# Sums of four steps for the softmax denominators, a part of the adds on VectorE, and the router's weight product moved, in a one-core attention and expert kernel

## The chip, the cores and the metric

The kernel runs on one core of a Trainium2 chip. The metric is the device time of one execution in microseconds (us), the median of several runs. TensorE multiplies matrices; VectorE, ScalarE and GpSimd work element by element, and SyncE issues the transfers (DMAs). Each engine has its own queue of instructions, worked off in order, and they meet only in semaphores.

## What is computed

A graph attention layer over 2048 nodes, then a causal attention of 16 heads, then a router and eight experts (the two best for each token). The part that matters here:

```python
scores = jnp.einsum('bhqd,bhkd->bhqk', q, k) / jnp.sqrt(jnp.float32(HD))
scores = jnp.where(causal, scores, -jnp.inf)
attn = jax.nn.softmax(scores, axis=-1)          # exp(s - max) / sum of them
y = jnp.einsum('bhqk,bhkd->bhqd', attn, v)
x = x + y @ w_o
logits = xf.astype(jnp.float32) @ w_router.astype(jnp.float32)   # xf: x, normed with g2
```

The layer norm ahead of the attention treats the 2048 rows as one sequence: 16 tiles of 128, 16 heads of 32 columns, 512 columns in all.

## The kernel before

**Stages.** `stage_sequence` (norm, x @ W_seq, the adjacency matrix turned), `stage_factors` (a short stage of small tiles), `stage_masks` (graph attention), `stage_front` (projections), `stage_attention`, `stage_slots` (who goes to which expert), `stage_experts`. A stage is one block: the next begins when every engine has ended its part.

**Attention.** The heads go in four quads of four. A quad has NS = 40 steps, in chunks c = 0 to 3 of 512 queries: chunk c has 4c + 4 steps, one for each 128 keys; its last four are the diagonal ones, whose columns begin at 0, 128, 256 and 384. In each step n TensorE makes the scores of step n + 1 in two halves z of two heads (`scores`, L1639 and L1642), ScalarE exponentiates them into one of three buffers E[n % 3] (L1407), and TensorE multiplies the values with E (`values`, L1653, four heads side by side in the array, two records each).

The denominator is the sum of E over all keys. GpSimd first adds the E of two steps, 2k and 2k + 1, into `total` (L1369; where the second step is narrower, a copy, L1368, takes over the first columns), and TensorE then multiplies `total` with ones (`denominators`, L1666), accumulating in one bank through a chunk. There is one `total`: GpSimd waits for `den_done` before the next pair. ScalarE's exponential into E[n % 3] waits until step n - 3 has been multiplied and summed. In the second half of the last quad VectorE makes the half z = 1 of the pair's add (`pair_sum`, L1535 and L1536).

**Score maxima.** The exponentials need the maximum of each row. TensorE makes the scores of a query tile against up to 512 keys (`entry`, L1622, with L1625 on the diagonal) in one of two banks, and VectorE takes the maximum (L1473). So TensorE may be two maxima ahead of VectorE. In steps 0 to 20 of a quad the maxima of its own later chunks are made, in steps 21 to 39 those of the next quad, some four a step (more in the first quad); TensorE spreads them around the two score halves: a quarter of them, scores z = 0, up to a half, scores z = 1, the rest, then `denominators`, then `values`. VectorE's queue has for each step: the maxima, the copy of a finished chunk (L1433), one part of a divide (a reciprocal, L1451, and a multiply, L1445, of 128 columns; five parts for each chunk, from four steps behind its end), then `pair_sum` where it is VectorE's.

**Last quad, second half.** No maxima are left. Behind steps 23 to 35 TensorE makes the output products and the router's (`router`: "out" L1699, "share" L1703, "sum" L1708) for 12 of 16 tiles, VectorE adds them up (L1482, L1486) and GpSimd adds the rows to the residual (`add_row`, L1356). Behind the last denominators product come four "out" jobs; the first needs the divide of the last chunk.

**Router's weight product.** The logits' weights are g2 times w_router; `stage_factors` multiplies them with w_o, in 16 products of 128 x 8 columns (L390), after its own transposes (L383), and ScalarE copies the result to WG (L367). Its inputs are the last DMAs of `stage_sequence`; GpSimd multiplies them with g2 (L325).

## Time and profile before

| | us |
|---|---|
| median of three runs | 2271.41 (2270.23 to 2273.5) |
| the profiled execution | 2268.96 |
| its span, first to last instruction | 2267.2 |
| TensorE busy | 2055.1 (91%) |
| VectorE busy | 1553.6 (69%) |
| ScalarE busy | 1078.9 (48%) |
| GpSimd busy | 584.4 (26%) |

One execution is recorded by the profiler. Busy shares are means over stages with different bounds, so each stage has to be read by itself. A product's line gives its duration from start to end; products overlap, so what one costs TensorE is the distance from its start to the next start. "idle before" tells how long an engine had nothing to do ahead of an instruction, and who ended that. The granted clock of TensorE is 1.00 at 2.4 GHz and 0.50 at 1.2 GHz.

### The profile page before, as it was taken

The page shows a single profiled execution, that of the slowest core. Times are in us where ns is not written, and L with a number is a line of the kernel's source. Part 1 is how long each engine was busy: PE and PEld are TensorE (multiplying, and loading weights), DVE is VectorE, ACT ScalarE, POOL GpSimd, SP SyncE. Part 2 cuts the span into 40 slices and gives each one's busy share as a digit, 9 for nine tenths or more (in the row PEclk, how much of TensorE's full clock was granted, in tenths as well). Part 3 has the DMA queues.
Part 4 walks back from the last instruction along what each step waited for, and adds up shares of the span by engine and source line. Part 5 has one row for each costly group of instructions (what it writes and reads, how often), then busy time and mean ns, then how long its engine had stood idle before and what let it go on. Part 6 is the DMA issues. An engine that isn't in the chain of part 4 may idle for free. (4 is left out here: it accounts for less than half of the span.)

```text
span 2267.2 us, 42225 instructions
## 1 busy us (share of the span) xinstructions
PE 2055.1 (91%) x17716; PEld 1213.2 (54%) x17716; DVE 1553.6 (69%) x2563; ACT 1078.9 (48%) x1059; POOL 584.4 (26%) x447
## 2 busy tenths in 40 slices
PE   6899999999996899989999999999991599999997
PEld 3554444444442344544444444444430599999997
DVE  6679999999984666757777778768347544444442
ACT  4868988989890333213444444444430233323331
POOL 2610000000002012333454555555340222222211
PEclk8989999999998999969999999999995699999999
DMA  6521212212115013343103121010203444444431
GB/s 227 182 79 51 72 52 74 69 52 78 49 52 199 25 47 102 130 112 72 36 16 87 31 64 49 20 38 10 80 24 130 158 121 121 121 121 121 116 66 24
DMA packets 90905, 185.87 MB, mean 82 GB/s; under 512 B 14332, under 2 KB 23548, under 8 KB 86332
## 3 DMA queue, kind: packets, MB, share of 16 engines
q1 hardware_dynamic: 81756, 162.20, 21.8%
q0 software_dynamic: 8960, 20.98, 5.0%
q8 instruction: 140, 2.29, 0.4%
q14 instruction: 49, 0.40, 0.1%
HBM read 138.47 MB, written 40.23 MB: 79 GB/s over the span
## 5 line engine op out<-in xcount | busy, mean ns | idle before, releaser
L1473 DVE TENSOR_REDUCE t_rm<-t_m 128x1 f32<-128x512 f32 (+3 forms) x640 | 372.8, 605 | 150.2 <-PE t_m L1622 96.8
L1407 ACT ACTIVATE t_E<-t_s 128x1024 f32<-128x1024 f32 (+3 forms) x320 | 277.4, 895 | 412.3 <-PE t_s L1639 223.8
L1369 POOL TENSOR_TENSOR t_total<-t_E 128x1024 f32<-128x1024 f32 (+2 forms) x151 | 292.4, 1947 | 221.4 <-PE t_d L1666 215.6
L573 ACT ACTIVATE m_step<-m_ub,gat_bias 128x2048 bf16<-128x2048 f32 x128 | 250.0, 1989 | 11.1 <-DMA m_ub<-scratch_uac 5.7
L715 PE MATMUL m_bd<-m_mask,m_S 128*32 128x512 bf16 x3072 | 230.4, 379 | 10.9 <-DVE m_mask L663 10.9
L715 PE MATMUL m_bd<-gat_adjT,m_S 128*32 128x512 bf16 x2496 | 201.4, 379 | 4.8 <-PE m_dn L715 4.8
L715 PE MATMUL m_bd<-m_mask,m_neg 128*32 128x512 bf16 x2496 | 189.0, 379 | 0.0
L1996 POOL DMA_INDIRECT out<-e_ye,e_token x40 | 80.7, 2018 | 339.1 <-DVE e_ye L2099 334.4
L2160 PE MATMUL e_h<-e_xTh,e_w1h 128*128 128x320 f32 x512 | 159.1, 311 | 1.4 <-DVE e_xTl L2080 1.4
L2160 PE MATMUL e_h<-e_xTh,e_w1l 128*128 128x320 f32 x512 | 158.8, 310 | 0.0
L2160 PE MATMUL e_h<-e_xTl,e_w1h 128*128 128x320 f32 x512 | 158.8, 310 | 0.0
L663 DVE TENSOR_TENSOR m_mask<-m_step,gat_adjT 128x2048 bf16<-128x2048 bf16 x128 | 153.3, 1219 | 4.0 <-PE m_dn L715 2.2
L1653 PE MATMUL t_o<-t_E,k_rows 128*32 128x512 f32 (+3 forms) x1280 | 153.2, 552 | 0.0
L900 POOL MEMSET k_triq<- 128x128 bf16 x1 | 0.2, 206 | 574.3 <-POOLq L2221 574.3
L2091 DVE SCALAR_TENSOR_TENSOR e_hTl<-e_h,e_hTh 128x320 fp32r<-128x320 f32 x128 | 62.7, 490 | 116.0 <-ACT e_hTh L2045 116.0
L715 PEld LDWEIGHTS m_bd<-m_mask,m_S 128*32 128x32 bf16 x3072 | 89.9, 96 | 95.3 <-DVE m_mask L663 25.2
L573 ACT ACTIVATE k_rows<-m_ub,gat_bias 128x2048 bf16<-128x2048 f32 x64 | 126.7, 1993 | 28.0 <-DVE m_mask L663 28.0
L573 ACT ACTIVATE gat_seq<-m_ub,gat_bias 128x2048 bf16<-128x2048 f32 x64 | 126.7, 1992 | 27.2 <-DVE m_mask L663 27.2
L1622 PE MATMUL t_m<-t_K,tq_Q 96*128 96x512 f32 (+3 forms) x288 | 121.5, 438 | 16.3 <-DVE t_rm L1473 14.1
L2179 PE MATMUL e_y<-e_w2h,e_hTh 128*128 128x512 f32 x320 | 127.5, 398 | 0.0
L2179 PE MATMUL e_y<-e_w2l,e_hTh 128*128 128x512 f32 x320 | 125.0, 391 | 0.0
L2179 PE MATMUL e_y<-e_w2h,e_hTl 128*128 128x512 f32 x320 | 124.7, 390 | 0.0
(359 smaller groups left out, 4085.7 us busy)
## 6 DMA issues: line engine op xcount, KB each, us to landing
a_adj<-in_adj SPq DMA_DIRECT2D x16, 1024.0 KB, 4.9
m_ub<-scratch_uac SPq DMA_DIRECT2D x16, 1024.0 KB, 5.0
e_w1r<-in_L_ffn_w SPq DMA_DIRECT2D x8, 2048.0 KB, 8.2
e_w2r<-in_L_ffn_w SPq DMA_DIRECT2D x8, 2048.0 KB, 8.8
tq_Q<-scratch_parts SPq DMA_DIRECT2D x36, 256.0 KB, 4.6
gat_scale<-scratch_uac SPq DMA_DIRECT2D x32, 256.0 KB
scratch_parts<-o_hi SPq DMA_DIRECT2D x32, 256.0 KB, 2.2
scratch_parts<-o_lo SPq DMA_DIRECT2D x32, 256.0 KB, 2.7
```

The costliest lines, as they stand in the source:

```text
L573: act.activation(step(n), ub[h % 2][:, :].rearrange("p (t q) -> p t q", t=T), ACT.Relu, bias=bias[:, j, h:h + 1], scale=BIG).then_inc(step ...
L663: dve.tensor_tensor(mask[n % MASKS][:, :].rearrange("p (t q) -> p t q", t=T), step(n), adjT[:, j, :].rearrange("p (t q) -> p t q", t=T), A ...
L715: return pe.matmul(out[c * TILE:(c + 1) * TILE, :], lhs, rhs[:, c * BANK:(c + 1) * BANK], **flags)
L1369: pool.tensor_tensor(total[:, two, off:BANK], E[a % 3][:, two, off:BANK], E[(a + 1) % 3][:, two, off:BANK], ALU.add).then_inc(summed[z], 1)
L1407: act.activation(E[n % 3][:, two, off:BANK], ps_s[:, two, off:BANK], ACT.Exp, scale=SCALE).then_inc(exp_done[z], 1)
L1473: dve.tensor_reduce(rm[:, h, t, ch:ch + 1], ps_m[i % 2][:, 0:w], AX, ALU.max).then_inc(entry_read, 1)
L1622: mm = pe.matmul(ps_m[i % 2][:, 0:w], Q[c][0:ROWS, h, t % 4 * P:(t % 4 + 1) * P], K[q % 2][ch][0:ROWS, h, 0:w], start=True, stop=not diag)
L1653: mm = pe.matmul(ps_o[h * DH:(h + 1) * DH, off:BANK], V[:, kt, (q * G + h) * DH:(q * G + h + 1) * DH], E[n % 3][:, h, off:BANK], start=(kt ...
L1996: pool.indirect_dma_start(out=out, out_offset=bass.IndirectOffsetOnAxis(ap=token[e % 3][:, s:s + 1], axis=0), in_=ye[s % 2][:, :], in_offs ...
L2091: dve.scalar_tensor_tensor(hT[1][:, f, cut], ps_h[n % 4][:, 0:HC], 0.0, hT[0][:, f, cut].bitcast(F32), ALU.max, ALU.subtract).then_inc(h_r ...
L2160: mm = pe.matmul(ps_h[n % 4][:, 0:HC], w1s[wp][:, k, f * P:(f + 1) * P], xT[xp][:, k, half * HC:(half + 1) * HC], start=(m == 0), stop=(m ...
L2179: mm = pe.matmul(ps_y[s % 2][:, :], hT[hp][:, f, s * P:(s + 1) * P], w2s[wp][:, f, :], start=(m == 0), stop=(m == 3 * FK - 1))
```

## The change

`denominators` now runs once for four steps, over the full 512 columns. The sum is built step by step: at the second step of a group of four the E of the first two are added into `total`, at the third and fourth E is added to `total`. The wait for `den_done` stands at the second step, and step 4k + 5 of TensorE holds the product of group k. VectorE makes the half z = 1 of the fourth step of each full group before step 144, at its place in step n + 1 (LAST_BY_VECTOR), and all halves z = 1 from step 144 on (BY_VECTOR). ScalarE's exponential waits for the sum up to step n - 3. GpSimd's row additions come a step later. Of the router's weight product, two of four column blocks move to the end of `stage_sequence`, behind a product with g2 that GpSimd now makes ahead of its products for tile 14, and a ScalarE copy; the third goes ahead of the first transposes of `stage_factors`, the fourth ahead of the transposes that wait for the exponentials. A PSUM bank of its own (`late`) holds these two.

```diff
@@ stage_sequence
+def router_columns(pe, keep, bank, k):
+    for b in range(KD):
+        mm = pe.matmul(bank[:, EXPERTS * k:EXPERTS * (k + 1)], keep["woT"][:, b, k * P:(k + 1) * P],
+                       keep["G"][:, b, :], start=(b == 0), stop=(b == KD - 1))
+    return mm
...
+                pool.memset(keep["WG"][:, :, :], 0.0).then_inc(g_ready, 1)
                 pool.wait_ge(a_in, 32)
                 for t in range(T - 1):
+                    if t == T - 2:
+                        pool.wait_ge(late_in, 16 * (KD + 2))
+                        pool.tensor_tensor(keep["G"][:, :, :], keep["G"][:, :, :],
+                                           keep["g2"][:, :, None].to_broadcast([P, KD, EXPERTS]),
+                                           ALU.mult).then_inc(g_ready, 1)
...
                 store(T - 1)
+                act.wait_ge(wg_early, WG_EARLY)
+                act.activation(keep["WG"][:, 0:WG_EARLY, 0:EXPERTS],
+                               ps_t[0][:, 0:WG_EARLY * EXPERTS].rearrange("p (k e) -> p k e", k=WG_EARLY), ACT.Copy)
...
                 turn(T - 1)
+                pe.wait_ge(g_ready, 2)
+                for k in range(WG_EARLY):
+                    router_columns(pe, keep, ps_t[0], k).then_inc(wg_early, 1)
@@ stage_factors
                     if n == 0:
+                        router_columns(pe, keep, late, WG_EARLY).then_inc(wg_full, 1)
                         pe.wait_ge(u_ready, 1)
                     if n == 2:
+                        for k in range(WG_EARLY + 1, KD):
+                            router_columns(pe, keep, late, k).then_inc(wg_full, 1)
                         pe.wait_ge(exp_done, 1)
...
-                pe.wait_ge(g_ready, KD + 3)
-                for k in range(KD):
-                    for b in range(KD):
...
@@ stage_attention
+    FOUR = 4
+    SUMS = []
+    for n in range(QUADS * NS):
+        first_pair = 2 if STEPS[n % NS - n % FOUR + 1][2] else 1
+        SUMS.append((SUMS[-1] if n else 0) + (first_pair, 0, 1, 1)[n % FOUR])
...
+    BY_VECTOR = range((QUADS - 1) * NS + HALF + FOUR, QUADS * NS)
+    LAST_BY_VECTOR = [n for n in range(BY_VECTOR.start) if n % FOUR == 3 and STEPS[n % NS][2] == 0]
...
+        def add_step(eng, n, z):
+
+            off, two = STEPS[n % NS][2], slice(2 * z, 2 * z + 2)
+            eng.wait_ge(exp_done[z], n + 1)
+            if n % FOUR == 1:
+                if n >= FOUR:
+                    eng.wait_ge(den_done, n // FOUR)
+                if off:
+                    eng.tensor_copy(total[:, two, 0:off], E[(n - 1) % 3][:, two, 0:off]).then_inc(summed[z], 1)
+                before = E[(n - 1) % 3]
+            else:
+                eng.wait_ge(summed[z], SUMS[n - 1])
+                before = total
+            eng.tensor_tensor(total[:, two, off:BANK], before[:, two, off:BANK],
+                              E[n % 3][:, two, off:BANK], ALU.add).then_inc(summed[z], 1)
...
+                for n in range(QUADS * NS):
+                    if n % FOUR:
+                        for z in range(1 if n in BY_VECTOR or n in LAST_BY_VECTOR else 2):
+                            add_step(pool, n, z)
+                    if n >= (QUADS - 1) * NS:
+                        while added < EARLY and STEP_OF[added] < n % NS - 2:
                             add_row(added)
                             added += 1
...
-                            act.wait_ge(summed[z], SUMS[(n - 3) // 2 + 1])
+                            act.wait_ge(summed[z], SUMS[n - 3])
...
-                        if s % 2 and (q * NS + s) // 2 in BY_VECTOR:
-                            pair_sum((q * NS + s) // 2)
+                        if q * NS + s - 1 in LAST_BY_VECTOR:
+                            add_step(dve, q * NS + s - 1, 1)
+                        if s % FOUR and q * NS + s in BY_VECTOR:
+                            add_step(dve, q * NS + s, 1)
...
-                        pe.wait_ge(summed[z], SUMS[k + 1])
+                        pe.wait_ge(summed[z], SUMS[FOUR * k + 3])
                     for h in range(G):
-                        mm = pe.matmul(ps_d[h * DH:(h + 1) * DH, off:BANK], ones[:, :], total[:, h, off:BANK],
-                                       start=(kt == 0), stop=last)
+                        mm = pe.matmul(ps_d[h * DH:(h + 1) * DH, :], ones[:, :], total[:, h, :],
+                                       start=(kt == 0), stop=(kt == 4 * c))
...
-                        if n >= 2 and n % 2 == 0:
-                            denominators(n // 2 - 1)
+                        if n > FOUR and n % FOUR == 1:
+                            denominators(n // FOUR - 1)
```

## Rows read from the trace of the kernel before

**Rows 1.** Busy time by stretch: span and length, then each engine, clock, DMA.

```profile
1228.00:1243.00 15.00, 12.94 (x92) 6.83 (x84) 13.57 (x23) 5.84 (x8) 6.43 (x8) 1.00 0.01 1
...
1276.00:1290.00 14.00, 13.80 (x113) 7.87 (x109) 8.04 (x18) 5.67 (x8) 6.43 (x8) 1.00 0.21 58
...
1005.00:1693.00 688.00, 645.92 (x3809) 308.83 (x3808) 479.63 (x846) 291.11 (x359) 326.76 (x223) 0.97 0.17 45
```

**Rows 2.** Timeline of TensorE (start, duration): a denominators and two values products.

```profile
1250.25 1.06 PE L1666 MATMUL t_d<-t_total,k_ones 128*32 128x512 f32 x8
1251.14 1.04 PE L1653 MATMUL t_o<-t_E,k_rows 128*32 128x512 f32 x8
...
1254.53 1.07 PE L1653 MATMUL t_o<-t_E,k_rows 128*32 128x512 f32 x8
```

**Rows 3.** Timeline of all engines, end of the attention's last quad.

```profile
1677.16 1.06 PE L1666 MATMUL t_d<-t_total,k_ones 128*32 128x512 f32 x8
...
1680.14 0.85 PE L1653 MATMUL t_o<-t_E,k_rows 128*32 128x384 f32 x8
...
1685.04 1.28 POOL L1356 TENSOR_TENSOR k_X<-k_X,t_rows 128x512 f32<-128x512 f32 x1
1685.13 0.64 PE L1666 MATMUL t_d<-t_total,k_ones 128*32 128x256 f32 x8 [1.60 <-POOL t_total L1369]
```

**Rows 4.** Groups by shape, GpSimd and VectorE, 1000 to 1740: busy, mean ns.

```profile
L1369 POOL TENSOR_TENSOR t_total<-t_E 128x1024 f32<-128x1024 f32 x90 | 212.8, 2383 | 221.4 <-PE t_d L1666 215.6 <-ACT t_E L1407 5.7
L1369 POOL TENSOR_TENSOR t_total<-t_E 128x768 f32<-128x768 f32 x31 | 57.2, 1845 | 0.0
L1368 POOL COPY t_total<-t_E 128x256 f32<-128x256 f32 x61 | 24.5, 402 | 148.2 <-PE t_d L1666 133.2 <-ACT t_E L1407 15.0
L1369 POOL TENSOR_TENSOR t_total<-t_E 128x256 f32<-128x256 f32 x30 | 22.4, 746 | 0.0
...
L1473 DVE TENSOR_REDUCE t_rm<-t_m 128x1 f32<-128x512 f32 x437 | 291.9, 685 | 108.7 <-PE t_m L1622 95.2 <-PE t_m L1625 8.3
L1451 DVE RECIPROCAL t_den<-t_den 128x128 f32<-128x128 f32 x64 | 60.4, 943 | 0.5 <-ACT t_den L1383 0.5
...
L1536 DVE TENSOR_TENSOR t_total<-t_E 128x1024 f32<-128x1024 f32 x6 | 7.3, 1210 | 0.0
```

**Rows 5.** Timeline of GpSimd: one pair's sum in two halves.

```profile
1251.43 4.72 POOL L1369 TENSOR_TENSOR t_total<-t_E 128x1024 f32<-128x1024 f32 x2 [2.87 <-PE t_d L1666]
```

**Rows 6.** The multiplies of line 1445: duration in ns, least, median, most.

```profile
L1445 DVE TENSOR_TENSOR t_out<-t_out,t_den x64: 279/282/1424, 1062.6 to 1691.0; 128x128 f32<-128x128 f32 x64
```

**Rows 7.** Timeline of all engines, end of stage_sequence, stage_factors, opening of stage_masks.

```profile
104.02 3.06 POOL L155 TENSOR_TENSOR a_prod<-gat_seq,a_row 128x512 f32<-128x512 f32 x2 [1.82 <-DVE s_s L216]
...
109.50 1.27 DVE L216 TENSOR_REDUCE s_s<-a_prod 128x16 f32<-128x512 f32 x2
...
112.19 0.28 PE L372 MATMUL f_p<-all_ident,f_pm 128*16 128x128 f32 x1 [4.96 <-DVE f_pm L332]
...
115.28 0.69 PE L383 MATMUL f_p<-all_ident,f_uac 128*128 128x128 f32 x2 [1.52 <-DVEq L343]
...
117.31 1.12 PE L383 MATMUL f_p<-all_ident,f_uac 128*128 128x128 f32 x4 [1.35 <-ACT f_uac L365]
...
118.01 6.95 PEld L390 LDWEIGHTS f_p<-all_marks,s_woT 128*128 128x128 f32 x32
...
119.64 0.37 SPq L400 DMA_DIRECT2D scratch_uac<-gat_scale  x1
...
125.54 0.33 SPq L504 DMA_DIRECT2D m_ub<-scratch_uac  x1
...
125.59 8.98 PE L703 MATMUL m_bd<-gat_adjT,gat_Dp 128*64 128x512 bf16 x64 [0.53 <-PEq L312]
```

**Rows 8.** Stretches of TensorE: length, busy (count), granted clock, DMA share, GB/s.

```profile
112.00:116.00 4.00, 1.54 (x5) 0.55 0.03 6
...
128.00:130.00 2.00, 2.00 (x14) 0.64 0.79 287
```

65 lines of the change are left out of this document (16 added, 49 removed).

## Prediction

> **What bounds the kernel now.** I first read the busy time by stretch [rows 1]. The attention stage lasts from 1005 to 1693 us; TensorE is busy for 645.9 of its 688 us, so 42 us of waiting is all that another engine can claim there. VectorE is busy for 480 us, but unevenly: in the stretch 1228 to 1243, where quotients are divided while score maxima are taken, it is busy 13.57 of 15 us against TensorE's 12.94, and in 1276 to 1290 only 8.04 of 14 against 13.80. TensorE is the bound with VectorE close behind: an addition to VectorE is free in the second kind of stretch and not in the first. Then I read TensorE in order of time through one step [rows 2]. From the start of one denominators product at full width (1250.25) to the values product behind it (1251.14) is 0.89 us; for one of 256 columns I take half, 0.45. A step without one takes 1254.53 - 1251.14 = 3.39 us, with one 4.28. These start-to-start gaps, not the 1.06 us that a line shows, are what TensorE loses, since the products overlap.
>
> **Denominators, the gain.** A quad has 40 steps, hence 20 pairs: 16 at full width, 4 at 256 columns. The change makes it 10 products of full width, over sums of four steps. Per full group of four, one product of 0.89 goes; per diagonal group, one full and one half become one full, so 0.45 goes. Up to the start of the product at 1677.16 [rows 3] that is 23 full groups, 15 diagonal ones, and one product more that is only moved later: 23 x 0.89 + 15 x 0.45 + 0.89 = 28.1 us, all taken from the engine that bounds the stage.
>
> **GpSimd.** Its full add takes 2.38 us [rows 4]. A full group had four, and now has six in three steps, of which it makes five: 11.9 us in a period of 3 x 3.39 + 4.28 = 14.5 us. It starts 0.29 us behind the values product (1251.43 against 1251.14) [rows 2, 5]. Counted from that product: step 4k+1 is summed at 5.0, 4k+2 at 9.8, its half of 4k+3 at 12.2, and the denominators product wants it at 13.6. The exponential of step 4k+5 now waits for the sum of 4k+2 (9.8); its scores of the second half stand at about 9.5. So 0.3 us is late there, on ScalarE, whose result is not wanted for two more us: nothing. Diagonal groups need two copies of 0.40 [rows 4], then adds of 1.85, a size not in the trace that lies between 0.75 and 1.85 (512 elements; I take 1.3, the middle) and 0.75, each twice: 8.6 us. GpSimd does not become the bound.
>
> **VectorE, the loss.** It gets 21 additional full adds before step 144 (six in each of the first three quads, three in the last), each 1.21 us by the six that it makes now [rows 4]. Each stands in its queue behind the maxima of step 4k+4 and in front of those of 4k+5, and TensorE may be only two maxima ahead, because there are two banks. Counted from the start of the values product of step 4k+4: values take 1.0, then come a maximum, scores, a maximum, scores, which is two thirds of the 2.4 us that a step of 3.39 leaves; so the third maxima product wants the bank of the first at about 2.5. VectorE has read the last maximum of 4k+4 at 0.7, makes the add until 1.9 and has read the next at 2.6 (a maximum is 0.67 [rows 4]): 0.1 late. With a reciprocal and a multiply of the divide between (0.94 and 0.28 [rows 4, 6]) it is 3.8, or 4.6 where the multiply meets GpSimd: 1.3 to 2.1 late. Divides stand at steps 3 to 12, 15 to 19 and 27 to 31 of a quad; the adds fall on steps 8, 16, 20, 28, 32 and 36. That makes 11 adds with a divide beside them and 10 without. I take 1.2 for the 11 (a little under the low end: the median of the multiplies is 0.28, and one maximum in four is narrower than 512) and 0.15 for the 10: 14.7 us. The bounds are 0 (all absorbed, as in 1276 to 1290) and, with a blocked multiply of 0.56 more by each add, 21 x 1.77 = 37. The nine adds of the last half quad replace six, beside output products for which VectorE waits: nothing.
>
> **Sharing of memory ports.** VectorE's multiply of 128 columns takes 0.28 us in most cases and up to 1.42 [rows 6]; the long ones fall where a GpSimd add runs. GpSimd's share of a full group grows from 9.5 of 15.3 us to 11.9 of 14.5, so more multiplies meet it: 64 multiplies, a fifth more of them met, 0.6 each is 8 us of VectorE, of which I put 1.5 on the path (it is VectorE-bound in about a fifth of the stage). Bounds 0 and 8. The Trainium skill (SBUF — State Buffer, "SBUF: two separate sides") says more: a VectorE instruction with two operands in SBUF and a GpSimd one that reads SBUF exclude each other for the whole instruction. It speaks against this change, which adds 21 such instructions; with the full GpSimd add to wait for, the multiply should reach 2.6 us, and the row's longest is 1.42, so I take the rule as true in kind and not in size; what it would make of the whole is a rival below.
>
> **The last group.** Before, TensorE's product at 1677.16, the values product of step 157 at 1680.14, the last denominators product at 1685.13, already waiting for GpSimd [rows 3]. After, the product before the last stands 0.89 ahead of where 1680.14 is, at 1679.25; GpSimd follows 1.18 later (1251.43 - 1250.25) at 1680.4. Then it works off copy 0.40, add 1.85, a row add 1.27, add 1.3, a row add 1.27, add 0.75 [rows 3, 4]: 1687.3 against 1685.13, and the last product has 512 columns instead of 256, 0.44 more. Loss 2.6 us; 0 if the row adds come early, 3.5 if the adds meet VectorE's. TensorE has then been idle for about 4.5 us. After the 4.96 us of idleness up to 112.19 the granted clock was 0.55 [rows 7, 8], which is its 1.2 GHz level; the four output jobs behind (16 products of 512 columns and two records each) would run slow for a while. I take 1.5 us of 0 to 4 (an estimate), because VectorE's queue covers part of it.
>
> **The router's product.** Now 32 weight loads and products stand alone from 118.01 to 124.96, the next stage's first DMA issues at 125.54, while the last other piece of work, SyncE's issue, is over at 120.01 [rows 7]. Two columns of the four go to the end of the first stage: TensorE is free from 107.23 (112.19 less 4.96), VectorE closes that stage at 110.77; two columns at 1.7 us or less end by 110.7 with ScalarE's short copy behind: nothing, at worst 0.2. GpSimd's small product with g2 now stands ahead of its products for tile 14, which start at 104.02; it costs at most 0.3 if the late loads, issued right behind the last block of adj, are there by then, and each us that they are later counts in full: I take nothing. The other two columns (1.7 us each, a quarter of 6.95) stand in gaps: one ahead of the transposes at 115.28, the next between 115.97 and 117.31. Together they push the second set of transposes by about 0.6, and SyncE's issue by 0.2. The next stage opens at 120.4 instead of 125.5: 5.1 us. Its 64 products (8.98 us) begin at the low clock either way, which rose 3.5 us into them (0.64 in 128 to 130 [rows 8]); without the run of small products before them the rise could come later: 0 to 4.5 us, I take 0 because the small products ran for 7 us without raising it. Bounds of this part 0.5 and 5.3.
>
> **Sum.** 28.1 - 14.7 - 1.5 - 2.6 - 1.5 + 5.1 = 12.9 us. The profiled execution took 2268.96 us with a span of 2267.2, so it would be 2256.1; the median of the three runs is 2271.41, 2.4 above it, and I predict for the median: 2258.5.
>
> **The rivals.**
> (A) The forecast, with losses on VectorE from 8 to 24 us instead of 16.2: 2250 to 2266. Chance 0.48.
> (B) VectorE absorbs nearly all: the maxima are read late, but TensorE's own queue of weights and products makes up for it. Then 28.1 - 1 - 2.6 + 5.1 = 29.6, 2242; with less loss at the end 2240. For it: TensorE waits only 42 us in this stage today. Against: the stretch 1228 to 1243. Chance 0.18.
> (C) Port exclusion of full size. An add of VectorE with no divide beside it is ready at 10.9, and GpSimd's half of step 4k+3 holds the ports until 12.2: 10 x 1.3, and 1 us for the 11 others, 14 us more than the forecast, 2272.5. The longest multiply [rows 6] speaks against it. Chance 0.14: no difference that can be told. This is what the rule of the Trainium skill's SBUF page named above would make of the change.
> (D) The clock of the stage behind the router's product rises late: 4.5 us less gain, 2263. Chance 0.09.
> (E) Slower: VectorE becomes the bound of the maxima. Each of the 21 adds is paid in full with one blocked multiply, 37 us; 2271.4 - 28.1 - 5.1 + 4.1 + 37 = 2279. It decides by the loss for one add: at 1.4 us the change is worth nothing, from 1.6 us on it is slower by more than can be missed. For it: VectorE's share of the stage rises from 70% to 75% (479.6 + 21 x 1.21 + 4, of 675), and in the stretches with divides it is at 90% already. Against: in the others it has 6 of 14 us free. Chance 0.11.
>
> **Chances and range.** A measurement can tell about 0.2% (4.5 us) from no change. Faster: A, B and D, 0.75; the same: C, 0.14; slower: E, 0.11. The range takes in A, B, D and C: 2240 to 2272.
>
> **What would show it.** In the changed profile: 40 denominators products of four heads instead of 80; GpSimd's adds at some 12 us per full group with idle time ended by TensorE's denominators product; steps of 3.39 us three times in four where VectorE has no divide; a wait of TensorE's maxima product of 0.5 to 1.5 us in steps 9, 17 and 29 of a quad; a wait for GpSimd's sum of over 4 us ahead of the last denominators product, and a granted clock below 1 behind it; the next stage's first DMA near 120.4. The prediction is wrong if TensorE's waits for the maxima grow by over 20 us, or if GpSimd's sums are what the denominators product waits for in every group.

## The result and the profile after

The changed kernel takes 2312.62 us (median, 2302.83 to 2320.64), beside 2271.52 for the kernel before in the same runs: a ratio of 1.0176, 95% interval 1.0151 to 1.0200. It is 41 us slower; the forecast was 2258.5, and its range ended at 2272. The profiled execution took 2311.2 us.

The busy time by stretch of the kernel after, as in [rows 1], but between the same two events in either kernel: the start of the attention's first values product, and of its last but one, that of step 158. First of after:

```profile
1003.74:1718.47 714.73, 652.10 (x3433) 310.99 (x3433) 526.06 (x844) 289.35 (x353) 408.57 (x242) 0.91 0.15 40
```

and the same of before:

```profile
1009.03:1682.70 673.67, 635.94 (x3753) 303.96 (x3756) 468.59 (x822) 288.21 (x355) 319.64 (x217) 0.97 0.17 43
```

Ahead of this stretch after is 5.3 us earlier (1003.74 against 1009.03); in it 41.1 us are lost (714.73 against 673.67). Behind that before has 584.5 of its span of 2267.2 us left and after 591.0 of 2309.5, so 6.5 us more go there. TensorE has 320 products fewer and is busy for 16 us more, at a granted clock of 0.91 instead of 0.97. VectorE is busy for 57 us more (forecast: 29 of adds and 8 of blocked multiplies), GpSimd for 89. Two rows of the page show where in the span the clock is lost, and the length of the whole (slices of 57 us before, 58 after; the attention is slices 18 to 30). First before, then after:

```profile
span 2267.2 us, 42225 instructions
...
PEclk8989999999998999969999999999995699999999
```

```profile
span 2309.5 us, 41744 instructions
...
PEclk9999999999997999958898999999996599999999
```

**One group of four.** All engines of after in order of time, from the values product of a step 4k + 1 to that of the step 4k + 5, the points from which the forecast's GpSimd sum counts; this answers [rows 2, 5]:

```profile
1267.38 1.04 PE L1673 MATMUL t_o<-t_E,k_rows 128*32 128x512 f32 x8
...
1267.74 4.71 POOL L1271 TENSOR_TENSOR t_total<-t_E 128x1024 f32<-128x1024 f32 x2 [9.01 <-PE t_d L1685]
...
1270.24 1.02 ACT L1436 ACTIVATE t_E<-t_s 128x1024 f32<-128x1024 f32 x1 [2.01 <-POOL t_total L1271]
...
1270.77 1.06 PE L1673 MATMUL t_o<-t_E,k_rows 128*32 128x512 f32 x8
...
1272.57 2.88 ACT L1436 ACTIVATE t_E<-t_s 128x1024 f32<-128x1024 f32 x3 [1.31 <-POOL t_total L1271]
...
1273.65 0.74 PE L1659 MATMUL t_s<-tq_Q,t_K 97*128 97x512 f32 x2 [0.67 <-ACT t_E L1436]
...
1274.85 1.07 PE L1673 MATMUL t_o<-t_E,k_rows 128*32 128x512 f32 x8
...
1279.52 0.94 DVE L1480 RECIPROCAL t_den<-t_den 128x128 f32<-128x128 f32 x1
...
1280.39 1.16 DVE L1271 TENSOR_TENSOR t_total<-t_total,t_E 128x1024 f32<-128x1024 f32 x1
...
1281.46 1.47 DVE L1502 TENSOR_REDUCE t_rm<-t_m 128x1 f32<-128x512 f32 x3
...
1282.19 0.33 PE L1642 MATMUL t_m<-t_K,tq_Q 96*128 96x128 f32 x1 [1.21 <-DVE t_rm L1502]
...
1283.22 1.07 PE L1685 MATMUL t_d<-t_total,k_ones 128*32 128x512 f32 x8
...
1284.11 1.04 PE L1673 MATMUL t_o<-t_E,k_rows 128*32 128x512 f32 x8
```

The group takes 16.7 us. The forecast said 14.5, and by [rows 2] the kernel before needs 15.3 (two steps of 3.39, two of 4.28). TensorE waits 0.67 us at 1273.65 for ScalarE, which itself waited for GpSimd's sum, and 1.21 us at 1282.19 for a maximum that VectorE could only take behind a reciprocal and the add. Over the whole stretch TensorE's own waits are these (total, times, longest), first before, then after:

```profile
PE t_m L1622 <- DVE t_rm L1473: 26.6, 62, 1.5
```

```profile
PE t_m L1642 <- DVE t_rm L1502: 38.9, 70, 2.4
PE t_s L1659 <- ACT t_E L1436: 13.0, 23, 1.3
```

The waits for the maxima grow by 12.3 us; the 13.0 us for ScalarE are new. Together they are the 25 us by which TensorE is idle for longer.

**A fall of the clock.** TensorE of after in order of time, and around it three stretches with the columns of [rows 1]:

```profile
1254.05 0.40 PE L1642 MATMUL t_m<-t_K,tq_Q 96*128 96x512 f32 x1
1255.39 0.74 PE L1659 MATMUL t_s<-tq_Q,t_K 97*128 97x512 f32 x2 [0.94 <-ACT t_E L1436]
1256.45 0.44 PE L1642 MATMUL t_m<-t_K,tq_Q 96*128 96x384 f32 x1 [0.32 <-DVE t_rm L1502]
...
1258.35 0.80 PE L1642 MATMUL t_m<-t_K,tq_Q 96*128 96x512 f32 x1
```

```profile
1253.00:1257.00 4.00, 2.71 (x16) 1.25 (x8) 3.99 (x5) 2.26 (x4) 4.00 (x4) 1.00 0.00 0
1257.00:1264.00 7.00, 6.95 (x26) 3.22 (x26) 5.66 (x10) 2.24 (x3) 1.73 (x3) 0.51 0.00 0
1264.00:1268.00 4.00, 3.81 (x29) 1.95 (x25) 2.27 (x4) 2.31 (x3) 0.26 (x1) 1.00 0.77 174
```

TensorE waits 0.94 and 0.32 us and is idle for 1.29 us of the first stretch; then its clock is 0.51, the level of 1.2 GHz, for 7 us in which it is busy without a gap. A maximum's product that took 0.40 us at 1254.05 takes 0.80 at 1258.35. In stretches of 0.5 us between 1036 and 1640, before has 4 such falls, each of 3.5 to 4 us, and after 15, of 3.5 to 11 us. The forecast had no term for this inside the stage: behind such waits come stretches of slow work, on top of the idle time. That the waits bring the falls about is read from their order and from the counts, not shown by a run that changes nothing else. The Trainium skill (TensorE: Matmul & The Clock Gate, "A second HAM failure mode: psum-queue depth-cycling") says of a kernel of bf16 products that short idle times of TensorE between groups of products, where it cycles through PSUM banks, make its clock go up and down. These rows, mostly of f32 products, agree: the maxima cycle through two banks.

**The accounting** below splits the attention's time in every kernel: from 996 us to its last exponential, in stretches of 4 us, TensorE's idle time is length minus busy time, and its time at 1.2 GHz is 2 x (1 - granted clock) x length, half of which is lost. What is left of the busy time is work at 2.4 GHz. Before: length 688, idle 39.4, low 48.2, hence work 688 - 39.4 - 24.1 = 624.5. After: length 724, idle 64.5, low 131.1, work 594.0. So 30.5 us of work went (forecast 28.1), and 25.1 us of idleness and 41.5 us lost to the low clock came. Since the kernels reach 996 us at different points and the last stretch is cut at whole 4 us, "work" is good to some 4 us. Between the two events above, in stretches of 2 us, it is 28.0 us less of work, 24.9 more of idleness and 44.1 more lost to the clock, which is the 41.1 us.

**The groups by shape** on VectorE, after, from 1000 to 1770 us, which answer [rows 4], and the multiplies' durations as in [rows 6]:

```profile
L1502 DVE TENSOR_REDUCE t_rm<-t_m 128x1 f32<-128x512 f32 x434 | 288.3, 684 | 105.5 <-PE t_m L1642 91.4 <-PE t_m L1645 9.5
L1480 DVE RECIPROCAL t_den<-t_den 128x128 f32<-128x128 f32 x64 | 60.3, 943 | 3.6 <-ACT t_den L1412 3.6
L1474 DVE TENSOR_TENSOR t_out<-t_out,t_den 128x128 f32<-128x128 f32 x64 | 46.0, 718 | 0.5 <-DVE t_m L1507 0.2
L1271 DVE TENSOR_TENSOR t_total<-t_total,t_E 128x1024 f32<-128x1024 f32 x27 | 38.1, 1411 | 1.3 <-DVE t_mT L1497 1.3
```

```profile
L1474 DVE TENSOR_TENSOR t_out<-t_out,t_den x64: 279/350/2539, 1059.6 to 1732.4; 128x128 f32<-128x128 f32 x64
```

The same 64 multiplies took 29.2 us before (here in its groups by shape):

```profile
L1445 DVE TENSOR_TENSOR t_out<-t_out,t_den 128x128 f32<-128x128 f32 x64 | 29.2, 457 | 0.5 <-DVE t_m L1478 0.2
```

**The last group**, all engines of after, which answers [rows 3]:

```profile
1716.82 0.83 PE L1673 MATMUL t_o<-t_E,k_rows 128*32 128x384 f32 x8
...
1724.43 0.71 POOL L1271 TENSOR_TENSOR t_total<-t_total,t_E 128x256 f32<-128x256 f32 x1
...
1725.20 1.93 PE L1685 MATMUL t_d<-t_total,k_ones 128*32 128x512 f32 x8 [3.62 <-POOL t_total L1271]
```

From step 157's values product to the last denominators product it is 8.4 us (1725.20 - 1716.82) against 5.0 before; the forecast had 8.05 (1687.3 - 1679.25). The product takes 1.93 us instead of 1.06, at a granted clock of 0.50. The forecast had no wait for the last exponentials, but ScalarE waits 3.64 us for GpSimd's sum there, and TensorE 1.97 us for ScalarE ahead of the last values product (at 1721.08).

**The router's product**, all engines of after, which answers [rows 7]:

```profile
105.23 1.90 PE L80 MATMUL a_t<-all_marks,s_woT 128*128 128x8 f32 x16
...
111.96 1.88 PE L80 MATMUL f_late<-all_marks,s_woT 128*128 128x8 f32 x8
...
114.14 1.72 PE L80 MATMUL f_late<-all_marks,s_woT 128*128 128x8 f32 x8
...
118.68 0.33 SPq L521 DMA_DIRECT2D m_ub<-scratch_uac  x1
```

The next stage's first DMA issues at 118.68 instead of 125.54, 6.9 us earlier where 5.1 were forecast. By the attention 5.3 of them are left: the stages between take 1.6 us more, at a granted clock of 0.96 instead of 0.97. A single trace scatters here. In the six kernels with the product at its old place the first values product starts at 1007.6 to 1011.2 us, 1009.1 in the mean; in the thirteen with the new place and nothing put ahead of the attention, at 1001.4 to 1008.6, 1004.4 in the mean. So the move is worth some 4.8 us there.

### The profile page after: what moved, and what is told of

Its sections match the earlier page's. It is cut to its first block and busy times, and to the rows that moved or that the text cites. A ratio compares the mean times of both kernels' runs of the same rounds, so it can differ in the third digit from the quotient of the medians.

```text
span 2309.5 us, 41744 instructions
## 1 busy us (share of the span) xinstructions
PE 2071.9 (90%) x17396; PEld 1219.1 (53%) x17396; DVE 1612.1 (70%) x2585; ACT 1080.5 (47%) x1060; POOL 675.2 (29%) x473
## 5 line engine op out<-in xcount | busy, mean ns | idle before, releaser
L1271 POOL TENSOR_TENSOR t_total<-t_total,t_E 128x1024 f32<-128x1024 f32 (+2 forms) x131 | 224.8, 1741 | 14.1 <-ACT t_E L1436 13.9
L1271 POOL TENSOR_TENSOR t_total<-t_E 128x1024 f32<-128x1024 f32 (+1 forms) x76 | 166.0, 2196 | 199.5 <-PE t_d L1685 199.5
L1673 PE MATMUL t_o<-t_E,k_rows 128*32 128x512 f32 (+3 forms) x1280 | 162.9, 583 | 2.5 <-ACT t_E L1436 2.0
```

Of the source, the lines that this page charges most:

```text
L1271: eng.tensor_tensor(total[:, two, off:BANK], before[:, two, off:BANK], E[n % 3][:, two, off:BANK], ALU.add).then_inc(summed[z], 1)
L1673: mm = pe.matmul(ps_o[h * DH:(h + 1) * DH, off:BANK], V[:, kt, (q * G + h) * DH:(q * G + h + 1) * DH], E[n % 3][:, h, off:BANK], start=(kt ...
```

## The experiments

Each run was timed in three rounds beside the kernel before (2268.7 to 2272.4 us). The kernel that an edit starts from is named with it. The runs were made on several chips, so they are compared by their ratios to the kernel before.

### The parts of the change

**router_only**: the kernel before with the change's edits in `stage_sequence` and `stage_factors` alone.

```diff
+                for k in range(WG_EARLY):
+                    router_columns(pe, keep, ps_t[0], k).then_inc(wg_early, 1)
...
+                        router_columns(pe, keep, late, WG_EARLY).then_inc(wg_full, 1)
```

> The kernel before with the router's weight product moved and the attention left as it was. From the trace of the changed kernel, whose third stage opens 6.9 us earlier at an unchanged length, I expect 5 to 7 us less than before, 2265, and the granted clock of the attention at 0.97 as before. If the loss of the change came from here (a clock that rises later in the stages behind), it would be slower than before.

Measured 2268.45, ratio 0.9990 (0.9975 to 1.0005): 2 us, where 5 to 7 were expected. The profiles show the gain at the start of the attention, but in the whole kernel it can't be told from nothing. So the loss comes with the attention's part of the change.

**no_vector**: the changed kernel, the 21 adds on GpSimd instead.

```diff
-    LAST_BY_VECTOR = [n for n in range(BY_VECTOR.start) if n % FOUR == 3 and STEPS[n % NS][2] == 0]
+    LAST_BY_VECTOR = []
```

> The changed kernel, but VectorE makes no add before step 144; GpSimd makes all six of a full group. Theory V (the 21 adds on VectorE delay the score maxima, and that is what the change costs): some 20 us or more faster than the changed kernel, 2290 or less. Theory W (ScalarE's exponential of step 4k+3 waits for GpSimd's first sum of the group, since its buffer held step 4k, and that sum starts only behind the denominators product of step 4k+1): no gain, since the first sum isn't touched, and the last half sum comes 2.4 us later: equal or up to 15 us slower, 2310 to 2325.

Measured 2340.75, 1.0306 (1.0219 to 1.0393): slower still, and outside what either theory had expected. With six adds in a group on GpSimd, 60 of VectorE's multiplies (up to 1740 us) take 63.8 us in all, where all 64 took 29.2 before. One of them shows more than any trace of before. GpSimd, VectorE and TensorE in order of time:

```profile
1107.72 9.25 POOL L1271 TENSOR_TENSOR t_total<-t_total,t_E 128x1024 f32<-128x1024 f32 x4
...
1107.96 9.17 DVE L1474 TENSOR_TENSOR t_out<-t_out,t_den 128x128 f32<-128x128 f32 x1
...
1118.59 0.79 PE L1642 MATMUL t_m<-first_K,tq_Q 96*128 96x512 f32 x1 [9.31 <-DVE t_rm L1502]
```

GpSimd's four adds stand back to back and end at 1116.97; the multiply of 0.28 us ends at 1117.13 and TensorE stands for 9.31 us. It was held not for one add but for all four. The same is seen behind three adds in a row in filler (6.89 us), no_fourth (6.85) and three_k (7.12), each ending 0.15 us behind the last add. The halves on VectorE hurt, and on GpSimd they hurt more.

**first_by_vector**: the changed kernel; VectorE makes its half at the second step of a full group instead of the fourth.

```diff
-    LAST_BY_VECTOR = [n for n in range(BY_VECTOR.start) if n % FOUR == 3 and STEPS[n % NS][2] == 0]
+    LAST_BY_VECTOR = [n for n in range(BY_VECTOR.start) if n % FOUR == 1 and STEPS[n % NS][2] == 0]
...
-                        if q * NS + s - 1 in LAST_BY_VECTOR:
-                            add_step(dve, q * NS + s - 1, 1)
+                        if q * NS + s in LAST_BY_VECTOR:
+                            add_step(dve, q * NS + s, 1)
```

> The changed kernel, but VectorE's add of a full group is the one of its second step (half z = 1) instead of the one of its fourth. VectorE has the same number of adds of the same size; the buffer that step 4k+3 wants is free some 2 us earlier. Theory W: ScalarE's waits for GpSimd (152 us in the changed kernel) fall by more than half, TensorE's waits for ScalarE (13 us) go, and the kernel gains 15 us or more, 2297 or less. Theory V: no gain, and as VectorE now also stands waiting for the denominators product in front of the next maxima, 0 to 20 us slower.

Measured 2330.85, 1.0268 (1.0248 to 1.0288). The place in the group is no remedy; theory V's "0 to 20 us slower" came. But the place changes something else too: the 21 adds now run beside GpSimd's and take 42.0 us in all, up to 3.08 each, where at the fourth step they take 24.9 and never over 1.23, and the 64 multiplies take 55.9 instead of 46.0. So this is no test of theory W alone.

**no_fourth**: the changed kernel without the 21 adds; VectorE's waits ahead of them stay.

```diff
                         if q * NS + s - 1 in LAST_BY_VECTOR:
-                            add_step(dve, q * NS + s - 1, 1)
+                            dve.wait_ge(exp_done[1], q * NS + s)
+                            dve.wait_ge(summed[1], SUMS[q * NS + s - 2])
+                            dve.sem_inc(summed[1], 1)
...
-                act.activation(den[u % 2][:, :], ps_d[:, :], ACT.Copy).then_inc(d_copied, 1)
+                act.activation(den[u % 2][:, :], ps_d[:, :], ACT.Copy, bias=1.0).then_inc(d_copied, 1)
```

> The changed kernel with VectorE's 21 adds before step 144 left out; its semaphores and waits stay. (Left out: half of the fourth step's sum in each full group; ScalarE adds 1 to the denominators.) It prices the adds alone, with GpSimd's load as in the changed kernel. Theory V: 20 us or more faster than the changed kernel, 2292. Theory C: the clock stays low for 100 us and more, and at most 15 us are gained, 2297 or more.

Measured 2279.78, 1.0050 (1.0034 to 1.0067). The adds cost 0.0126 of 2271.5, 29 us (33 by the medians), or 1.4 to 1.6 us each: more than their own 1.19 us. But without them the kernel is still 11 us slower than before, and by the forecast's sum it should have been 28 us faster (28.1 - 1.5 - 2.6 - 1.5 + 5.1).

**before_vector_adds**: the kernel before; VectorE makes two idle adds of 512 columns where the change puts its add.

```diff
+                        if (n0 := q * NS + s - 1) % 4 == 3 and n0 < (QUADS - 1) * NS + HALF + 4 and STEPS[n0 % NS][2] == 0:
+                            for i in range(2):
+                                lk(dve.tensor_tensor(square[:, :], V[:, 2 * i, :], V[:, 2 * i + 1, :], ALU.add))
```

> The kernel before with idle adds on VectorE (two of 512 columns into a scratch tile, 1.3 us together) at the 21 places where the changed kernel has its own. Sums and denominators products as before. The forecast's second step priced this at some 15 us, so 2284; theory C says that with all 80 products in place the clock holds, so 2270 to 2280.

Measured 2355.4, 1.0357 (1.0319 to 1.0395): 81 us, where the forecast's way of counting gave 15 and theory C under 9. The line's durations (least, median, most):

```profile
L1561 DVE TENSOR_TENSOR t_square<-k_rows x42: 681/2110/2808, 1063.9 to 1678.2; 128x512 f32<-128x512 f32 x42
```

Such an add takes 0.68 us alone and 2.11 at the median, because here GpSimd's adds of 2.38 us run beside it. It is blocked, not slowed: see the next run. So the 81 us are the price of adds that meet GpSimd's, not of adds as the changed kernel has them.

### Less work on TensorE alone

**half_denominators**: the kernel before; every second denominators product has 16 columns instead of 512 or 256 (most of the second pair's sum is left out).

```diff
+                    end = BANK if k % 2 == 0 else off + 16
...
-                        mm = pe.matmul(ps_d[h * DH:(h + 1) * DH, off:BANK], ones[:, :], total[:, h, off:BANK],
+                        mm = pe.matmul(ps_d[h * DH:(h + 1) * DH, off:end], ones[:, :], total[:, h, off:end],
...
-                act.activation(den[u % 2][:, :], ps_d[:, :], ACT.Copy).then_inc(d_copied, 1)
+                act.activation(den[u % 2][:, :], ps_d[:, :], ACT.Copy, bias=1.0).then_inc(d_copied, 1)
```

> The kernel before, with 16 columns instead of 512 or 256 in the denominators product of every second pair, so most of the work that the change takes from TensorE is gone while every add, wait and queue stays. (Left out: most of the second pair's sum; ScalarE adds 1 to the denominators to keep them above zero.) By the forecast's first step TensorE's queue is the bound, so some 24 us go: 2246. Theory C (TensorE's clock falls where it has less to do, waits or not): the low-level time in the attention rises from some 45 us to 80 or more, and half of that rise is paid, so it gains less than 10 us, 2260 or more.

Measured 2288.98, 1.0079 (1.0054 to 1.0103): 18 us slower, where the forecast's first step gave 24 us faster, although nothing was added anywhere and TensorE's work fell by 23.5 us (table below). The multiplies show where a large part of that comes from. Here is one in half_denominators with GpSimd's add beside it, then one of before, each in order of time:

```profile
1221.89 4.72 POOL L1369 TENSOR_TENSOR t_total<-t_E 128x1024 f32<-128x1024 f32 x2 [5.71 <-PE t_d L1667]
...
1222.18 2.21 DVE L1445 TENSOR_TENSOR t_out<-t_out,t_den 128x128 f32<-128x128 f32 x1
```

```profile
1157.28 4.72 POOL L1369 TENSOR_TENSOR t_total<-t_E 128x1024 f32<-128x1024 f32 x2 [4.33 <-PE t_d L1666]
...
1160.99 1.17 DVE L1445 TENSOR_TENSOR t_out<-t_out,t_den 128x128 f32<-128x128 f32 x1
```

GpSimd's row holds two adds of 2.36 us. In the first case the first of them ends at 1224.25 and the multiply, started 0.29 us behind it, at 1224.39; in the second the second add ends at 1162.00 and the multiply at 1162.16. Both multiplies end some 0.15 us behind an add: they waited for all that was left of it. Whether 0.28 becomes 1.2 or 2.2 us goes by when the multiply comes (and by how many adds stand in a row, see no_vector). Before, it happened to come late or between adds. Here, where only the denominators products are shorter, the 64 multiplies take 46.7 us against 29.2.

**filler**: the changed kernel with idle products of four heads back on TensorE, of the length of the removed ones, at the fourth step of a group.

```diff
+                        if n % FOUR == 3 and (own < upto or coming < later):
+                            turn_q, i = (q, own) if own < upto else (q + 1, coming)
+                            pe.wait_ge(entry_read, turn_q * NE + i - 1)
+                            for h in range(G):
+                                pe.matmul(ps_m[i % 2][h * DH:(h + 1) * DH, :], ones[:, :], V[:, h, :],
+                                          start=True, stop=True)
```

> The changed kernel with one group of four products more in each step 4k+3 in which maxima are made: same shape as a denominators product, written into the bank of the next maximum, which overwrites it, so TensorE has about as many products as before the change. Theory C (with fewer products TensorE's clock falls more often, 127 us at the low level in the attention against 44, and that is most of the loss): the time at the low level falls to under 80 us, and the kernel is no slower than the changed one in spite of 30 groups x 0.89 = 27 us and more of added work, perhaps 10 us faster. If the clock has no part in it, or falls because of waits alone, it is slower by up to 27 us, or the same where the filler lies in waits.

Measured 2310.47, 1.0185 (1.0163 to 1.0207). TensorE has 32.8 us more of work than in the changed kernel and takes no longer: the time at 1.2 GHz falls from 131 to 76 us. That is what theory C had expected. What the change took from TensorE was given up again, most of it to the clock.

**half_filler**: half_denominators with such products, ahead of a step's maxima.

```diff
+                        if n % 4 == 0 and n and (own < upto or coming < later):
...
+                                pe.matmul(ps_m[i % 2][h * DH:(h + 1) * DH, :], ones[:, :], V[:, h, :],
+                                          start=True, stop=True)
```

> The kernel before with the second pair's denominators product cut to 16 columns (2289 us, 20 slower than before), and in the same steps, where maxima are made, a group of four products of full width put back as a mere filler, ahead of the maxima, into the bank that the next maximum overwrites. (Left out: most of the second pair's sum.) It has more work on TensorE than the kernel with the cut. Theory C (the clock pays for the missing products): the time at the low clock falls from 102 to some 50 us and the kernel is faster than the cut one by 10 us or more, under 2279. Rival (the cut shifts the order of the queues): no faster, or slower by the filler's 20 us.

Measured 2321.52, 1.0220 (1.0195 to 1.0244). Idleness grows from 51.7 to 54.7 us and the time at 1.2 GHz from 103 to 121, where theory C had expected some 50. That the clock simply follows the amount of work on TensorE is refuted; it matters where the work stands. That the filler does harm here because it delays VectorE's next maximum was argued, not shown.

**start_filler**: router_only with idle products ahead of the first scores and in the first four steps, where the clock is low.

```diff
+                        if n < 4 and (own < upto or coming < later):
...
+                                pe.matmul(ps_m[i % 2][h * DH:(h + 1) * DH, :], ones[:, :], V[:, h, :],
+                                          start=True, stop=True)
```

> The kernel before with the router's product moved, and six filler groups of four dense products in TensorE's queue at the beginning of the attention's steps (two ahead of the first scores, one in each of steps 0 to 3), where the clock stands at its low level from 972 to 1020 us although TensorE is busy. Theory C: the clock rises some 15 us earlier, which gives back up to 7 us, less the filler's own 5 to 10 us: 2262 to 2272. If fillers don't lift the clock: 2275 or more.

Measured 2269.51, 0.9993 (0.9982 to 1.0004). The low time goes from 38 to 19 us, and the filler's own work takes what that gives.

### GpSimd's sum and the waits for it

**early_skip**: the changed kernel; the part of a divide that would stand in a step with VectorE's add is moved out of it, and the denominators product stands ahead of the step's last maxima.

```diff
-                        if turn:
+                        if turn and q * NS + s - 1 not in LAST_BY_VECTOR:
...
-                        if n > FOUR and n % FOUR == 1:
-                            denominators(n // FOUR - 1)
+                            if g == 1 and n > FOUR and n % FOUR == 1:
+                                denominators(n // FOUR - 1)
```

> The changed kernel with two shifts: the denominators product of group k stands ahead of the last maxima of step 4k+5 instead of behind them (0.9 us earlier, so the first sum of the next group and the exponential of step 4k+3 are earlier), and VectorE makes no part of a divide in a step in which it makes an add. Theory W (waits of ScalarE for the first sum, and of TensorE for maxima behind VectorE's add): TensorE's idle time in the attention falls from 64 us to 50 or less, the time at the low clock falls too, and the kernel is 15 us or more faster than the changed one, under 2297. Rival (the loss is in the fewer products alone): no difference over 5 us.

Measured 2321.07, 1.0224 (1.0198 to 1.0250). ScalarE's waits for the sum fall from 149 us to 113, TensorE's weight loads wait for maxima 192 us instead of 154, and the 64 multiplies take 60.0 us instead of 46.0. Some 11 us slower than the changed kernel, the intervals just touching, where theory W had expected 15 faster and its rival no difference over 5.

**three_k** (the changed kernel with three blocks of `K1` instead of four, to make room) and **three_k_two_totals** (the same with two buffers `total`, used in turn: the first add of a group doesn't wait for the denominators product of the one before).

```diff
-        K1s = st.sb("K1", [P, NC, G, BANK], F32R)
+        K1s = st.sb("K1", [P, NC - 1, G, BANK], F32R)
...
-        total = st.sb("total", [P, G, BANK])
+        totals = [st.sb(f"total{i}", [P, G, BANK]) for i in range(2)]
...
-                    eng.wait_ge(den_done, n // FOUR)
+                    eng.wait_ge(summed[z], SUMS[n - 2])
+                if n >= 2 * FOUR:
+                    eng.wait_ge(den_done, n // FOUR - 1)
```

> Control for the next run: the changed kernel, in which the key buffer of quads 1 and 3 has three chunks instead of four, the fourth chunk using the third's keys. (So the scores of a part of the keys are those of others; queues and waits are the same, two times three loads are left out.) As the changed kernel within 3 us: 2310.

> The control with the memory so freed used for a second sum buffer: the first add of a group waits no longer for the denominators product of the group before, only for that group's last add. Adds, products and VectorE's share are unchanged. Theory W: ScalarE's waits for GpSimd (152 us) nearly vanish, TensorE's for ScalarE (13 us) too, and since its clock then falls less, 20 us or more are gained against the control, 2290 or less. Theory V (VectorE's adds are the cost): TensorE's waits for the maxima stay at 40 us and under 10 us are gained. Theory C alone: nothing is gained.

Measured 2313.06, 1.0166 (1.0119 to 1.0212), and 2319.73, 1.0211 (1.0183 to 1.0238). ScalarE's waits for GpSimd's sum fall from 149 us to under 1 in the second, and nothing is gained: idleness is 72.0 and 73.4 us. TensorE meets VectorE instead; among other things the 64 multiplies take 64.6 us there against 51.4 in three_k.

### With VectorE relieved

**before_no_multiply**, **half_no_multiply**, **no_fourth_no_multiply**, **after_no_multiply**: the kernel before, half_denominators, no_fourth and the changed kernel, each with

```diff
-                        dve.tensor_tensor(out[u % 2][:, part], out[u % 2][:, part], den[u % 2][:, part],
-                                          ALU.mult).then_inc(normed, 1)
+                        dve.sem_inc(normed, 1)
```

> The kernel before without the 64 multiplies of the divide on VectorE (left out: the product of the output with the reciprocal of the denominator; the reciprocals stay). It is the base for the two runs beside it. Theory V (VectorE is the second bound of the score maxima; TensorE's stalls behind it bring its clock down): VectorE has 29 us less to do, TensorE's waits for the maxima shrink from 27 us to some 20 and the stretches at a low granted clock from 48 us to some 30: 2271 - 7 - 9 = 2255 (2248 to 2265). Theory K (the clock goes by the number of products alone): TensorE's products are the same, the low stretches stay, only 7 us of waits go: 2264.

> half_denominators (the kernel before with every second denominators product cut to 16 columns, ScalarE adding 1 to the denominators so that they stay above zero) and without the 64 multiplies of the divide (left out, as in before_no_multiply). Against before_no_multiply it has some 25 us less of products on TensorE and nothing else. Theory V: VectorE has room, so TensorE's saving pays in good part: 10 to 20 us below before_no_multiply, about 2240. Theory K: the clock falls as often as in half_denominators, and the kernel lies 10 to 18 us above before_no_multiply, about 2278.

> The changed kernel without VectorE's 21 halves of the fourth step before step 144 (left out of the sum) and without the 64 multiplies of the divide (left out). Against before_no_multiply: one denominators product for four steps, and GpSimd's adds. Theory V: 10 to 25 us below before_no_multiply, about 2235 to 2245. Theory K: at or above before_no_multiply, as no_fourth is 8 us above the kernel before: 2265 to 2275.

> The changed kernel without the 64 multiplies of the divide on VectorE (left out). They take 44 us of VectorE in its attention, against 29 us in the kernel before, where leaving them out gained 13.7 us of time. Theory V (VectorE's load decides, whatever it is made of): the gain is more than in the kernel before and more than in proportion to their length, since stalls of TensorE bring its clock down: 25 to 35 us, 2278 to 2288. Rival P (only an add that stands between two maxima hurts, the multiplies have their own gaps): the gain is that of the kernel before, 10 to 15 us, 2298 to 2303.

Measured 2258.72, 0.9952 (0.9932 to 0.9973); 2254.71, 0.9929 (0.9906 to 0.9952); 2269.70, 0.9991 (0.9977 to 1.0005); 2289.24, 1.0060 (1.0037 to 1.0084). The multiplies cost 11 us in the kernel before (1 - 0.9952), 26 in the changed one (1.0176 - 1.0060) and 34 in half_denominators (1.0079 - 0.9929). With them half_denominators is 18 us slower than its base, without them 5 us faster (intervals overlapping): the multiplies, blocked for longer, are 23 us of that difference (give or take 9, by the four intervals) and more than all of its loss. The expected 10 to 20 us of gain against before_no_multiply didn't come: against before_no_multiply TensorE has 25 us less of work, 8 us more of idleness and 34 us more at 1.2 GHz. For this run theory K is refuted as stated (no loss of 10 to 18 us), and theory V's gain is not clear of noise. no_fourth_no_multiply is 9 us slower than before_no_multiply: theory V had expected 10 to 25 us faster, and the time lies where theory K put it (2265 to 2275). ScalarE still waits 157 us for GpSimd's sums in it, against under 1 in half_no_multiply; the next run removes those waits. before_no_multiply lies within theory V's range (2248 to 2265), but no farther from theory K's 2264 than from V's 2255, and its low time fell to 43 us, not to 30. after_no_multiply gained 26 us, as theory V had it (25 to 35).

**two_totals_no_multiply**: no_fourth_no_multiply with the two buffers of three_k_two_totals (the same edit as there).

> no_fourth_no_multiply (left out: the half z = 1 of the fourth step in 21 groups, and the divide's 64 multiplies) with two buffers for the total, used in turn by the groups, so that the first add of a group no longer waits for the denominators product of the group before (the room comes from a fourth block of K1, which costs nothing by three_k). Against it, in its trace: TensorE's 15 us of waits for ScalarE at the first scores, ScalarE's 157 us of waits for the sum. Theory W (with VectorE relieved, these waits are what keeps the shorter TensorE work from paying): they go, and the time falls by 10 to 17 us to 2253 to 2260, where half_no_multiply is. Rival (as in the changed kernel, where the same edit gained nothing, because TensorE then meets VectorE): 2265 to 2275.

Measured 2265.34, 0.9967 (0.9950 to 0.9985), 5 us below no_fourth_no_multiply, intervals overlapping, where 10 to 17 were expected. In its trace TensorE's 15.1 us of waits for ScalarE are gone and idleness falls from 50.3 to 40.7 us; but the time at 1.2 GHz grows from 73 to 93. The missed wait is real and worth little.

**gp_multiply**: router_only; GpSimd makes the multiplies of all chunks but the last two, two behind each pair's sum.

```diff
+                def multiply(u, r):
+                    part = slice(r * BANK // 4, (r + 1) * BANK // 4)
+                    pool.wait_ge(inverted, u * 4 + r + 1)
...
+                    pool.tensor_tensor(out[u % 2][:, part], out[u % 2][:, part], den[u % 2][:, part],
+                                       ALU.mult).then_inc(normed, 1)
...
+                    for r0, back in ((0, 5), (2, 7)):
+                        m0 = a - back
+                        if m0 >= 0 and m0 % NS in END.values():
+                            u = m0 // NS * NC + STEPS[m0 % NS][0]
+                            if u < FROM_VECTOR:
+                                multiply(u, r0)
+                                multiply(u, r0 + 1)
...
+                        if u < FROM_VECTOR:
+                            return recip(u, r)
```

> The kernel before with the router's product moved as in the change (worth nothing by router_only) and the divide's multiplies of the chunks before the last two made by GpSimd, between its pair sums; all of the computation is there. Theory V: VectorE loses 25 us of work, multiplies held up by GpSimd among them; GpSimd gains 56 multiplies of some 0.4 us or 22 us and has 220 us of idle time: 2255 to 2266. Rival G (GpSimd's sums come later by two or four multiplies, 0.8 to 1.6 us, in the steps of a divide, and the denominators product or ScalarE waits for them): 2270 to 2285. Theory K: no difference, 2266 to 2271.

Measured 2258.84, 0.9942 (0.9921 to 0.9964): faster than both kernels, 13 us below the kernel before and 11 below router_only, its own base, with everything computed. That is what leaving the multiplies out altogether gained (11 us). GpSimd's multiplies (least, median, most):

```profile
L1383 POOL TENSOR_TENSOR t_out<-t_out,t_den x56: 445/457/478, 1061.3 to 1570.2; 128x128 f32<-128x128 f32 x56
```

On one engine with the adds they can't meet them: 0.46 us each and never more, where VectorE's took 0.28 to 1.42 [rows 6].

### The accounting of all of them

In us; "work", "idle" and "low" as defined above, from one profiled execution each, so that a few us between two rows say nothing; "change" is the ratio of the timed runs minus 1, times 2271.5. The profiled execution was 13 us above its median in no_fourth, 15 below in no_vector, 4 to 7 below in router_only, two_totals_no_multiply, gp_multiply, start_filler, early_skip and half_denominators, and within 3 in the others.

| | change | work | idle | low |
|---|---|---|---|---|
| before | 0 | 624.5 | 39.4 | 48 |
| router_only | -2 | 621.8 | 39.4 | 38 |
| start_filler | -2 | 630.2 | 40.2 | 19 |
| gp_multiply | -13 | 618.7 | 29.6 | 39 |
| before_no_multiply | -11 | 620.9 | 29.4 | 43 |
| half_no_multiply | -16 | 595.7 | 37.8 | 77 |
| two_totals_no_multiply | -7 | 588.6 | 40.7 | 93 |
| no_fourth_no_multiply | -2 | 593.2 | 50.3 | 73 |
| no_fourth | +11 | 591.8 | 57.5 | 117 |
| after_no_multiply | +14 | 595.9 | 59.8 | 97 |
| half_denominators | +18 | 601.0 | 51.7 | 103 |
| after | +40 | 594.0 | 64.5 | 131 |
| filler | +42 | 626.8 | 59.5 | 76 |
| early_skip | +51 | 594.1 | 65.4 | 145 |
| half_filler | +50 | 624.9 | 54.7 | 121 |
| first_by_vector | +61 | 591.5 | 65.8 | 181 |
| no_vector | +70 | 588.9 | 76.2 | 150 |
| before_vector_adds | +81 | 612.6 | 80.7 | 157 |

By and large the low time rises with the idle time. It isn't fixed by it: near 40 us of idleness it is 48 in before and 93 in two_totals_no_multiply, near 60 it is 76 in filler and 97 in after_no_multiply. Less work on TensorE goes with more low time in these two pairs, but not in half_filler against half_denominators (121 and 103, with 24 us more of work).

## Why the prediction was wrong

**What bounds the kernel now.** Right as far as it went: TensorE with VectorE close behind. The step that failed is the sentence that 42 us of waiting is all that another engine can claim, and with it the passage from work taken off TensorE to time gained. Idle time was 39 us and the low clock took another 24; the change brought 25 us more of the one and 44 of the other.

**Denominators, the gain.** Right as work: 28.1 us forecast, 28.0 less of work between the same two events. Wrong as time: half_denominators takes 23.5 us of the same work away and is 18 us slower.

**GpSimd.** The sizes were right, the narrow adds among them (1.28 us by the trace, 1.3 taken). The queue was followed from one denominators product to the next and one consumer was left out of the term that was put at nothing: the exponential of step 4k + 3, which overwrites the E of step 4k and so waits for the group's first add, which waits for the denominators product. ScalarE's waits for the sum are 149 us in the trace, TensorE's for ScalarE 13.0, half of its new idleness. That "nothing" was wrong, but taking these waits away gains little (two_totals_no_multiply: about 5 us with VectorE relieved, intervals overlapping; three_k_two_totals: none).

**VectorE, the loss.** 14.7 us forecast; 29 to 33 measured by no_fourth. The single wait was forecast well (0.1 to 2.1 us late; 1.21 in the group shown). What was mis-sized is what such a wait costs in all: 1.4 to 1.6 us for an add of 1.19, instead of 0.7. The traces put it half to idleness and half to the clock (57.5 and 117 in no_fourth, 64.5 and 131 in after), but the execution profiled for no_fourth was a slow one of its kind, so the split isn't shown. It is nearly the deciding point that rival E named.

**Sharing of memory ports.** This is the other failed step. "True in kind and not in size" was read off the longest multiply of before, 1.42 us. But that multiply ended with GpSimd's add: its length says when it came, not how long it can be held. The runs showed multiplies of 2.2 and 2.5 us, idle adds of 2.8, and where GpSimd's adds stand in a row, multiplies of 6.9 to 9.2. The rule of the Trainium skill (SBUF — State Buffer, "SBUF: two separate sides"), that the two exclude each other for a whole instruction, agrees with these traces in full size; behind a row of adds the hold lasted to the end of the row. 16.8 us more of VectorE's time came of it (8 forecast), and taking the multiplies out of the changed kernel gives 26 us, against 11 before: some 15 us (give or take 9) on the path instead of 1.5. Rival C took the rule for the adds, which were never held (the 21 took at most 1.23 us), and missed what the shift of the multiplies does. Its 2272.5 also lay just outside the range that was to take it in.

**The last group and the clock behind it.** The mechanism and the wait are right (8.4 us against 8.05 forecast), but the wait ahead of the last values product was missed (1.97 us); 6.5 us more from step 158's values product on, where some 4 were forecast.

**The router's product.** Right in mechanism. That 5.3 us at the attention is so near to the forecast 5.1 is partly luck: 6.9 us were gained at the next stage and 1.6 lost behind it, where a fall of 0 to 4.5 us had been considered and put at nothing. In the whole kernel it can't be told from nothing (0.9990, interval down to 0.9975, or 6 us), a point that stays open.

**The two signs of being wrong.** Neither showed: TensorE's waits for the maxima grew by 12.3 us, not by over 20, and of the 40 denominators products only the last waited for GpSimd's sum (3.6 us). The prediction was wrong all the same, through what its signs didn't watch: the clock, and ScalarE.

**The rivals.** E was right in sign, and too small: 2279 against 2312.6. It had VectorE's adds paid in full and one blocked multiply with each, 37 us, and kept the 28.1 of the denominators as gain. half_denominators shows that this gain was not there to have: cutting those products alone makes the kernel 18 us slower. Without them GpSimd's adds meet the multiplies at another phase (46.7 us instead of 29.2). That the product was also cover under which VectorE caught up fits TensorE's waits for the maxima, 37 us there against 27, but wasn't tested by itself.

**What stays open.** With VectorE relieved and GpSimd's sums as before (half_no_multiply), 25 us less of work still give only 5. Idle time and the low clock take the rest; 7 of the 8 us of idleness are waits for the maxima (24.7 us against 18.0), so VectorE's remaining work is in it, but why they come with 34 us at 1.2 GHz wasn't settled. No run holds the clock fixed, so how much of the 41 us is the clock's doing, and how much only comes along with the waits, is told by the accounting alone.

## What to carry to other kernels

Work taken off the busiest engine is not yet time gained: cut the work alone, as half_denominators did, before building what makes the cut possible. Where two engines hand each other two banks, ask whether the other has room at that very place. If a VectorE instruction is now and then longer beside GpSimd, compare its end with the end of GpSimd's: if they coincide, it is blocked outright, and a shift of phase can make it as long as GpSimd's, or as a whole row of GpSimd's that stand back to back. Where GpSimd has time to spare, as here, short instructions of VectorE with two SBUF operands can go to GpSimd itself, behind its own adds: gp_multiply gained 11 us by it.
